# A slot plan for two-way state-space scans: work beside the scans is re-dated, two spare rows go, and GpSimd's order and share change

## The chip, the cores and the metric

The kernel runs on one core of a Trainium2 chip. The metric is the device time of one launch in microseconds. The kernel before took 6414.39 us in the median of three runs (6395.42 to 6419.84). A launch is a whole small network; the change touches one of its nine stages, the state-space layer, which holds about 1900 us of the launch.

The engines are called as the profile calls them: PE is TensorE, DVE VectorE, ACT ScalarE, POOL GpSimd, SP the queue that issues most DMAs.

## The reference

The reference runs a bidirectional Mamba layer (and eight other stages that are not touched) over 32 sequences of 113 tokens with 256 features. Cut to what matters here, for each of the two directions:

```python
xz = x @ in_w.T;  xh, z = split(xz, 2)                  # 512 inner channels each
xc = silu(conv_b + sum(shift(xh, k) * conv_w[:, k] for k in range(4)))
proj = xc @ xproj_w.T                                   # dt (16), B (16), C (16)
delta = softplus(dt @ dt_w.T + dt_b)
dA  = exp(delta[..., None] * A)                         # A = -exp(A_log), 16 states
dBu = (delta * xc)[..., None] * B
h_t = dA_t * h_(t-1) + dBu_t                            # the recurrence, per channel and state
y_t = sum over the 16 states of h_t * C_t
out = ((y + xc * D) * silu(z)) @ out_w.T
```

## The kernel before, in words

Features lie on the 128 partitions. The 32 sequences go in 8 groups of 4, so one row has GT = 4 x 113 = 452 columns. The 512 inner channels make IB = 4 blocks. A group is worked in two *halves*, direction 0 and direction 1, so there are 16 halves, numbered 0 to 15 here; even ones have direction 0. They run in two blocks of code (halves 0 to 7 and 8 to 15), ahead of which a short block prepares the first one.

A half has 16 states of 4 scans each: 64 *slots*. Slot i is block ORDER[i % 4] (0, 2, 1, 3) of state i // 4. Its parts, with the names of the code:

- `decays` (ACT, L1386): dA of the slot, into one of two PSUM banks. ACT can be two slots ahead of the scans.
- `input_terms` (POOL, L1459): dBu = du x B for two blocks at once, 904 columns; two of them a state. That of state n + 1 may begin when the third scan (blocks 0, 1) or the fourth (2, 3) of state n - 1 is done, as dBu has two buffers.
- `recur` (DVE, L1519): the scan. The result of blocks 0 and 1 goes to `hs` in SBUF (two buffers), that of blocks 2 and 3 to one PSUM bank.
- the output products, state x C: blocks 2 and 3 by DVE (`output_term`, L1529), blocks 0 and 1 by POOL (`output_terms`, L1468), 904 columns. A scan into `hs` waits until the product of the state two before is done.
- `product` (PE, L1297): adds the output product to y in PSUM through the identity, in the order of blocks 2, 3, 0, 1: that of state n - 1 at slots 4n to 4n + 3.
- SP loads the rows B and C of a state, broadcast to all partitions, into a ring of four.

Beside the scans, at slots that constants set, each engine does the work that surrounds the recurrence (`beside`). For the half that comes next: X_MM (PE), the convolution's first tap (ACT, TAP), three more taps (DVE), Z_MM (PE), Z_RAW (ACT copies z out of PSUM), SILU twice (ACT: table load, silu of xc, silu of this half's z, table load back), XP_MM and ROWS (B, C and dt), and then four times DT_MM (PE), softplus in three ACT steps, STEP (DVE) and, on POOL, `step_input` (du, L1475). All of these share a single PSUM bank, XZ. For the half before: GATE (DVE), OUT_MM (PE), RES (DVE). Odd halves also normalise the next group (MEAN, CENTRE, SQUARE, VAR, RSTD, SCALE). Every engine takes its list strictly in order, so what waits at a slot holds all later slots of that engine. The last half has no half to prepare.

While ACT is at SILU it can't make dA. Before, two *spare rows* in SBUF (`dA_spare`) are filled ahead of each SILU, for the two slots behind it. So four scans of a half read dA from SBUF; their other operand, dBu, is in SBUF too.

## Time and profile before

| | us |
|---|---|
| median of the runs | 6414.39 |
| the profiled execution's own time | 6388.95 |
| its span | 6387.2 |
| PE busy in the span | 5081.8 |
| DVE busy | 3776.1 |
| ACT busy | 2136.6 |
| POOL busy | 2244.7 |
| the 16 halves: start of the first scan to the end of the last | 1514.8 to about 3341 |

The page gives busy times over all nine stages. Only in the stretch from about 1500 to 3340 us does the changed code run, so shares of the whole span tell little; the rows further down are of that stretch, most of them from two halves in its middle: half 4 (even), whose first scan starts at 1969.87 us, and half 5 (odd), 2085.86 to 2198.63.

### The profile page before, as it was taken

To read this page: it belongs to the slowest core of one execution; us is meant where nothing else is said; L and a number is where in the kernel's file an instruction comes from. 1 tells how busy PE (TensorE), PEld (TensorE's weight loads), DVE (VectorE), ACT (ScalarE), POOL (GpSimd) and SP (SyncE) were. 2 spreads that over 40 slices of the span, in tenths; PEclk is the share of its full clock that TensorE was granted. 3 is DMA by queue.
4 is the path that set the end of the run, shared out by engine and by line. 5 is a ranking of instruction groups with operands and counts; after the bars stand their busy time and mean duration, and the time that the engine had idled before them with its cause. 6 is when DMAs were issued, how large, how long until landed. Compare 5 with 4: busy or idle time off the path is not lost. (4 is left out here: it accounts for less than half of the span.)

```text
span 6387.2 us, 65263 instructions
## 1 busy us (share of the span) xinstructions
PE 5081.8 (80%) x21148; PEld 3347.0 (52%) x21148; DVE 3776.1 (59%) x7281; ACT 2136.6 (33%) x3642; POOL 2244.7 (35%) x1326
## 2 busy tenths in 40 slices
...
DMA packets 154586, 290.22 MB, mean 45 GB/s; under 512 B 24422, under 2 KB 136082, under 8 KB 145520
## 3 DMA queue, kind: packets, MB, share of 16 engines
...
q8 instruction: 115, 1.88, 0.1%
...
## 5 line engine op out<-in xcount | busy, mean ns | idle before, releaser
L1297 PE MATMUL ssm_ps<-ssm_hc,net_ident 128*128 128x452 f32 x2048 | 989.2, 610 | 288.6 <-DVE ssm_hc L1529 236.7
L1459 POOL TENSOR_TENSOR ssm_dBu<-ssm_du,ssm_bc 128x904 f32<-128x904 f32 x512 | 1098.9, 2167 | 21.3 <-DMA ssm_bc<-ssm_rows 11.2
L1297 PEld LDWEIGHTS ssm_ps<-ssm_hc,net_ident 128*128 128x128 f32 x2048 | 399.3, 209 | 827.9 <-DVE ssm_hc L1529 414.0
L1386 ACT ACTIVATE ssm_ps<-ssm_step,ssm_decay 128x448 f32<-128x448 f32 x960 | 597.7, 633 | 639.5 <-DVE ssm_ps L1519 406.9
L2724 POOL TENSOR_TENSOR peer_hot_cols<-peer_hot_cols,peer_codesT 128x512 f32<-128x512 f32 (+1 forms) x240 | 285.4, 1189 | 1162.1 <-DVE peer_hot_cols L2740 1162.1
L1519 DVE TENSOR_TENSOR_SCAN ssm_ps<-ssm_ps,ssm_dBu 128x452 f32<-128x452 f32 x480 | 528.9, 1102 | 115.2 <-ACT ssm_ps L1386 56.4
L1468 POOL TENSOR_TENSOR ssm_hc<-ssm_hs,ssm_bc 128x904 f32<-128x904 f32 x256 | 538.9, 2105 | 89.6 <-DVE ssm_hs L1519 89.4
L1519 DVE TENSOR_TENSOR_SCAN ssm_hs<-ssm_ps,ssm_dBu 128x452 f32<-128x452 f32 x480 | 517.3, 1078 | 56.4 <-ACT ssm_ps L1386 32.1
L2634 PE MATMUL peer_ps<-peer_xn,peer_down 128*128 128x226 f32 x2048 | 452.9, 367 | 23.2 <-issue 16.0
L2737 DVE TENSOR_TENSOR peer_hot_rows<-peer_ramp,peer_codesT 128x1024 f32<-128x1024 f32 (+1 forms) x240 | 282.6, 1177 | 284.2 <-PE peer_ps L2649 254.1
L2649 PEld LDWEIGHTS peer_ps<-peer_hot_cols,peer_hot_rows 128*128 128x128 f32 x3616 | 437.8, 193 | 23.8 <-DVE peer_hot_rows L2737 22.4
L2649 PE MATMUL peer_ps<-peer_hot_cols,peer_hot_rows 128*128 128x64 f32 x3616 | 429.1, 273 | 18.5 <-DVE peer_hot_rows L2737 18.5
L2676 PE MATMUL peer_ps<-peer_hid,peer_up 128*128 128x226 f32 x2048 | 399.7, 355 | 1.5 <-DVE peer_hid L2756 1.5
L2634 PEld LDWEIGHTS peer_ps<-peer_xn,peer_down 128*128 128x128 f32 x2048 | 382.9, 195 | 29.2 <-issue 24.1
L2676 PEld LDWEIGHTS peer_ps<-peer_hid,peer_up 128*128 128x128 f32 x2048 | 390.0, 190 | 6.7 <-issue 2.1
L1529 DVE TENSOR_TENSOR ssm_hc<-ssm_ps,ssm_bc 128x452 f32<-128x452 f32 x512 | 307.5, 601 | 0.0
L418 POOL TENSOR_TENSOR at_ex<-at_ex,at_rs 113x452 f32<-113x452 f32 x128 | 125.3, 982 | 447.7 <-DVE at_rs L470 447.7
L2703 ACT ACTIVATE peer_hid<-peer_ps 128x452 f32<-128x452 f32 x256 | 140.0, 547 | 414.7 <-PE peer_ps L2634 414.7
L2696 ACT ACTIVATE peer_weight<-peer_ps 128x512 f32<-128x512 f32 (+1 forms) x240 | 144.3, 609 | 288.3 <-PE peer_ps L2649 288.3
...
L2421 POOL IOTA peer_ramp<- 128x128 f32 x1 | 0.2, 237 | 636.6 <-ACTq L2410 636.6
L2049 POOL MEMSET rw_back<- 128x4520 f32 x1 | 3.9, 3864 | 592.9 <-POOLq L73 592.9
...
## 6 DMA issues: line engine op xcount, KB each, us to landing
ssm_bc<-ssm_rows SPq DMA_DIRECT2D x256, 452.0 KB, 3.6
...
```

Source lines behind the costliest of these rows:

```text
L1297: nc.tensor.matmul(Y_BANK[j][:, 0:GT], c["ident"][:, :], hc[:, q % 2, j, :], start=False, stop=(n == S - 1))\
L1386: nc.scalar.activation(rows(dA(place[i]))[:, :, lo:lo + N - 1], rows(step[hf.d][:, j, :])[:, :, lo:lo + N - 1], ACT.Exp, scale=decay[hf.d] ...
L1459: nc.gpsimd.tensor_tensor(dBu[:, q % 2, j:j + 2, :], du[hf.d][:, j:j + 2, :], bc[:, q % RING, 0:1, :].to_broadcast([P, 2, GT]), ALU.mult). ...
L1468: nc.gpsimd.tensor_tensor(hc[:, q % 2, 0:2, :], hs[:, q % 2, :, :], bc[:, q % RING, 1:2, :].to_broadcast([P, 2, GT]), ALU.mult).then_inc(s ...
L1519: nc.vector.tensor_tensor_scan(flow(state, hf.d), flow(dA(place[i]), hf.d), flow(dBu[:, q % 2, j, :], hf.d), 0.0, ALU.mult, ALU.add).then_ ...
L1529: nc.vector.tensor_tensor(hc[:, q % 2, j, :], HS_BANK[:, 0:GT], bc[:, q % RING, 1, :], ALU.mult)\
L2634: mm = nc.tensor.matmul(ps[1 + i % 3][:, jj * PT:(jj + 1) * PT], down[:, m, i * J + jj, :], xn[:, m, :], start=(m == 0), stop=(m == DK - 1))
L2649: mm = nc.tensor.matmul(ps[4 + ch % HB][:, t * PB * EB:(t + 1) * PB * EB], hot_rows[:, at % HB, t, :], hot_cols[:, at % HB, t, :], start=T ...
L2676: mm = nc.tensor.matmul(ps[5 + m][:, 0:PT], w_up[:, j, m * P:(m + 1) * P], hid[:, j, :], start=(j == 0), stop=(j == EB - 1))
L2696: nc.scalar.activation(weight[:, :, :, t0:t0 + n], ps[4 + ch % HB][:, 0:n * PB * EB].rearrange("p (t b j) -> p j b t", b=PB, j=EB), ACT.Co ...
L2724: nc.gpsimd.tensor_tensor(hot_cols[:, at % HB, 0:n, :], hot_cols[:, at % HB, 0:n, :], codesT[:, 2, t0:t0 + n].unsqueeze(2).to_broadcast([P ...
L2737: nc.vector.tensor_tensor(hot_rows[:, at % HB, 0:n, :], ramp[:, :].unsqueeze(1).to_broadcast([P, n, P]), codesT[:, 0, t0:t0 + n].unsqueeze ...
```

## The change

Six things change, all in `mamba`.

1. The constants: nearly all beside work gets another slot. GATE moves from 2, 3, 5, 6 to 2, 3, 4, 5; OUT_MM from 8, 11 to 6, 9; RES from 10, 13 to 9, 12; X_MM from 14 + 7m to 13 + 6m; TAP from 16 + 7m to 15 + 6m; Z_MM from 19 + 7m to 16 + 6m; Z_RAW from 21 + 7m to 18 + 6m; SILU from 30, 41 to 27, 36; XP_MM from 44 to 38; DT_MM from 47 + 4m to 42 + 4m; STEP from 50 + 4m to 45 + 4m.
2. `dA_spare` goes. The slots alternate between the two PSUM banks, and ACT works them in their order.
3. The three DVE taps of a block, one a slot before, are issued at one slot.
4. Softplus' three ACT steps, one behind another at one slot before, get a slot each (ABS, EXP, LOG).
5. POOL does the two input products of state n + 1 ahead of the output product of state n - 1, and `step_input` follows states 12 and 14.
6. The output products of states 5, 7 and 8 for blocks 0 and 1 are DVE's (`output_pair`, at slots 26, 35, 36), and PE waits for them on a semaphore of their own, `hc_own`.

```diff
-    MEAN, CENTRE, SQUARE, VAR, RSTD, SCALE = -1, 1, 3, 5, 7, 9
-    GATE = (2, 3, 5, 6)
-    OUT_MM, RES = (8, 11), (10, 13)
-    X_MM = [14 + 7 * m for m in range(IB)]
...
+    MEAN, CENTRE, SQUARE, VAR, RSTD, SCALE = -1, 0, 2, 3, 5, 8
+    GATE = (2, 3, 4, 5)
+    OUT_MM, RES = (6, 9), (9, 12)
+    X_MM = [13 + 6 * m for m in range(IB)]
+    TAP = [15 + 6 * m for m in range(IB)]
+    Z_MM = [16 + 6 * m for m in range(IB)]
+    Z_RAW = [18 + 6 * m for m in range(IB)]
+    SILU = (27, 36)
+    XP_MM, ROWS = 38, 40
+    DT_MM = [42 + 4 * m for m in range(IB)]
+    ABS, EXP, LOG = ([42 + k + 4 * m for m in range(IB)] for k in (1, 2, 3))
+    STEP = [45 + 4 * m for m in range(IB)]
+    DU = {12: 0, 14: 2}
+    PAIR_SLOT = {26: 5, 35: 7, 36: 8}
+    OWN = sorted(PAIR_SLOT.values())
...
+        def pairs(q):
+            own = q // S * len(OWN) + sum(n <= q % S for n in OWN)
+            return q + 1 - own, own
+        def pair_wait(eng, q):
+            pool, own = pairs(q)
+            if q % S in OWN:
+                eng.wait_ge(s["hc_own"], own)
+            else:
+                eng.wait_ge(s["hc_pool"], pool)
...
                         if j < 2:
-                            pe.wait_ge(s["hc_pool"], q + 1)
+                            pair_wait(pe, q)
...
                         for n in range(S):
-                            if hf.rec and n:
-                                output_terms(hf, n - 1)
-                            elif hf.carried is not None:
-                                output_terms(hf.carried, S - 1)
                             if hf.rec and n + 1 < S:
                                 input_terms(hf, n + 1, 0)
                                 input_terms(hf, n + 1, 2)
...
+                            if hf.rec and n:
+                                if n - 1 not in OWN:
+                                    output_terms(hf, n - 1)
+                            elif hf.carried is not None:
+                                output_terms(hf.carried, S - 1)
+                            if n in DU and hf.front:
+                                step_input(hf, DU[n])
...
+                    def output_pair(hf, n):
+                        q = S * hf.r + n
+                        dve.wait_ge(s["scan_done"], IB * q + AT[1] + 1)
+                        if q >= 2:
+                            dve.wait_ge(s["y_pool"], 2 * (q - 1))
+                        nc.vector.tensor_tensor(hc[:, q % 2, 0:2, :], hs[:, q % 2, :, :],
+                                                bc[:, q % RING, 1:2, :].to_broadcast([P, 2, GT]), ALU.mult).then_inc(s["hc_own"], 1)
```

The lists show three places. On PE, around the fourth Z_MM of a half, before (`ssm_w_in` at L1343 is Z_MM, `net_ident` is `product`, waiting for `hc_dve` or `hc_pool`):

```order
L1297 MATMUL ssm_ps<-ssm_hc,net_ident 128x452 [waits ssm_hc_pool] x2
L1297 MATMUL ssm_ps<-ssm_hc,net_ident 128x452 [waits ssm_hc_dve]
L1343 MATMUL ssm_ps<-ssm_ln_out,ssm_w_in 128x452 [waits ssm_conv_step]
L1343 MATMUL ssm_ps<-ssm_ln_out,ssm_w_in 128x452
L1297 MATMUL ssm_ps<-ssm_hc,net_ident 128x452 [waits ssm_hc_dve]
```

and in the changed kernel (Z_MM is L1348, `product` L1302; the X_MM in front of it is L1341):

```order
L1341 MATMUL ssm_ps<-ssm_ln_out,ssm_w_in 128x452 [waits ssm_z_raw]
L1341 MATMUL ssm_ps<-ssm_ln_out,ssm_w_in 128x452
L1302 MATMUL ssm_ps<-ssm_hc,net_ident 128x452 [waits ssm_hc_dve] x2
L1302 MATMUL ssm_ps<-ssm_hc,net_ident 128x452 [waits ssm_hc_own]
L1348 MATMUL ssm_ps<-ssm_ln_out,ssm_w_in 128x452 [waits ssm_conv_step]
L1348 MATMUL ssm_ps<-ssm_ln_out,ssm_w_in 128x452
L1302 MATMUL ssm_ps<-ssm_hc,net_ident 128x452 [waits ssm_hc_own]
```

The fourth Z_MM now stands behind a product that waits for DVE's own pair of state 7, which DVE issues at slot 35.

On ACT, around the second SILU, before (L1386 is `decays`, L1408 is Z_RAW):

```order
L1386 ACTIVATE ssm_ps<-ssm_step,ssm_decay 128x4x112 [waits ssm_scan_done] x4
L1386 ACTIVATE ssm_dA_spare<-ssm_step,ssm_decay 128x4x112 [waits ssm_scan_done] x2
L1413 ACT_TABLE_LOAD [waits ssm_conv_step]
L1413 ACTIVATE ssm_xc<-ssm_conv 128x904
L1418 ACTIVATE ssm_z<-ssm_z 128x904
L1420 ACT_TABLE_LOAD
L1408 ACTIVATE ssm_z<-ssm_ps 128x452 [waits ssm_z_mm]
```

and now (`decays` is L1391, Z_RAW L1413):

```order
L1391 ACTIVATE ssm_ps<-ssm_step,ssm_decay 128x4x112 [waits ssm_scan_done] x3
L1413 ACTIVATE ssm_z<-ssm_ps 128x452 [waits ssm_z_mm]
L1418 ACT_TABLE_LOAD [waits ssm_conv_step]
L1418 ACTIVATE ssm_xc<-ssm_conv 128x904
L1423 ACTIVATE ssm_z<-ssm_z 128x904
L1425 ACT_TABLE_LOAD
L1391 ACTIVATE ssm_ps<-ssm_step,ssm_decay 128x4x112 [waits ssm_scan_done] x4
```

The fourth Z_RAW has moved from behind the second SILU to ahead of it, and nothing is made ahead for the slots behind.

On POOL, from the end of state 4 on, before (L1459 are inputs, L1468 outputs):

```order
L1468 TENSOR_TENSOR ssm_hc<-ssm_hs,ssm_bc 128x904 [waits ssm_y_pool,ssm_scan_done]
L1459 TENSOR_TENSOR ssm_dBu<-ssm_du,ssm_bc 128x904 [waits ssm_scan_done,ssm_landed2] x2
L1468 TENSOR_TENSOR ssm_hc<-ssm_hs,ssm_bc 128x904 [waits ssm_y_pool,ssm_scan_done]
L1459 TENSOR_TENSOR ssm_dBu<-ssm_du,ssm_bc 128x904 [waits ssm_scan_done,ssm_landed3] x2
L1468 TENSOR_TENSOR ssm_hc<-ssm_hs,ssm_bc 128x904 [waits ssm_y_pool,ssm_scan_done]
L1459 TENSOR_TENSOR ssm_dBu<-ssm_du,ssm_bc 128x904 [waits ssm_scan_done,ssm_landed0] x2
```

and now (L1464 inputs, L1473 outputs):

```order
L1464 TENSOR_TENSOR ssm_dBu<-ssm_du,ssm_bc 128x904 [waits ssm_scan_done,ssm_landed2] x2
L1473 TENSOR_TENSOR ssm_hc<-ssm_hs,ssm_bc 128x904 [waits ssm_y_pool,ssm_scan_done]
L1464 TENSOR_TENSOR ssm_dBu<-ssm_du,ssm_bc 128x904 [waits ssm_scan_done,ssm_landed3] x2
L1464 TENSOR_TENSOR ssm_dBu<-ssm_du,ssm_bc 128x904 [waits ssm_scan_done,ssm_landed0] x2
L1473 TENSOR_TENSOR ssm_hc<-ssm_hs,ssm_bc 128x904 [waits ssm_y_pool,ssm_scan_done]
```

Each output now follows the two inputs that it led before, and where DVE has taken a pair, four inputs stand together.

## Rows read from the trace of the kernel before

**Rows 1.** Busy time by engine: halves 4, 5 and 15 (PE, PEld, DVE, ACT, POOL, clock).
```profile
1969.87:2085.86 115.99, 89.83 (x201) 38.17 (x202) 104.08 (x122) 60.53 (x94) 103.96 (x51) 0.91 0.21 65
2085.86:2198.63 112.77, 91.89 (x208) 38.90 (x206) 103.97 (x126) 62.60 (x97) 106.46 (x51) 0.94 0.21 67
3236.18:3341.00 104.82, 73.18 (x152) 30.30 (x152) 96.53 (x108) 48.12 (x70) 102.03 (x49) 0.89 0.18 58
```
**Rows 2.** The page's costliest groups: busy, mean ns | idle before, by releaser.
```profile
L1459 POOL TENSOR_TENSOR ssm_dBu<-ssm_du,ssm_bc 128x904 f32<-128x904 f32 x512 | 1098.9, 2167 | 21.3 <-DMA ssm_bc<-ssm_rows 11.2
...
L1519 DVE TENSOR_TENSOR_SCAN ssm_ps<-ssm_ps,ssm_dBu 128x452 f32<-128x452 f32 x480 | 528.9, 1102 | 115.2 <-ACT ssm_ps L1386 56.4
```
**Rows 3.** Scans from the spare rows into PSUM: ns min/median/max.
```profile
L1519 DVE TENSOR_TENSOR_SCAN ssm_ps<-ssm_dA_spare,ssm_dBu x32: 2202/2660/8458, 1563.7 to 3309.6; 128x452 f32<-128x452 f32 x32
```
**Rows 4.** Timeline (start, us, engine) of half 4, state 11, DVE and POOL.
```profile
2055.89 1.10 DVE L1519 TENSOR_TENSOR_SCAN ssm_hs<-ssm_ps,ssm_dBu 128x452 f32<-128x452 f32 x1 [0.86 <-ACT ssm_ps L1386]
...
2057.07 2.10 POOL L1468 TENSOR_TENSOR ssm_hc<-ssm_hs,ssm_bc 128x904 f32<-128x904 f32 x1 [0.84 <-DVE ssm_hs L1519]
...
2057.64 1.11 DVE L1519 TENSOR_TENSOR_SCAN ssm_ps<-ssm_ps,ssm_dBu 128x452 f32<-128x452 f32 x1
...
2060.38 1.11 DVE L1519 TENSOR_TENSOR_SCAN ssm_ps<-ssm_ps,ssm_dBu 128x452 f32<-128x452 f32 x1
```
**Rows 5.** Timeline: first scans of states 4, 6 and 10 of half 4, and state 4 of half 5.
```profile
1997.47 1.07 DVE L1519 TENSOR_TENSOR_SCAN ssm_hs<-ssm_ps,ssm_dBu 128x452 f32<-128x452 f32 x1
...
2010.31 1.09 DVE L1519 TENSOR_TENSOR_SCAN ssm_hs<-ssm_ps,ssm_dBu 128x452 f32<-128x452 f32 x1
...
2044.48 1.08 DVE L1519 TENSOR_TENSOR_SCAN ssm_hs<-ssm_ps,ssm_dBu 128x452 f32<-128x452 f32 x1
...
2115.57 1.07 DVE L1519 TENSOR_TENSOR_SCAN ssm_hs<-ssm_ps,ssm_dBu 128x452 f32<-128x452 f32 x1
```
**Rows 6.** Timeline of half 4 around a scan from a spare row.
```profile
2018.33 4.21 POOL L1459 TENSOR_TENSOR ssm_dBu<-ssm_du,ssm_bc 128x904 f32<-128x904 f32 x2
...
2021.59 6.01 DVE L1519 TENSOR_TENSOR_SCAN ssm_ps<-ssm_dA_spare,ssm_dBu 128x452 f32<-128x452 f32 x1
...
2024.49 2.14 POOL L1459 TENSOR_TENSOR ssm_dBu<-ssm_du,ssm_bc 128x904 f32<-128x904 f32 x1
```
**Rows 7.** The norm's DVE product of two SBUF rows, 904 columns: ns min/median/max.
```profile
L142 DVE TENSOR_TENSOR ssm_ln_out<-ssm_ln_centred,ssm_ln_rstd x8: 1100/2709/2721, 1442.1 to 3025.5; 128x904 f32<-128x904 f32 x8
```
**Rows 8.** Timeline of half 5: a tap, a product, Z_MM and Z_RAW after an idle PE.
```profile
2145.79 0.66 DVE L1538 SCALAR_TENSOR_TENSOR ssm_conv<-ssm_ps,ssm_conv_w,ssm_conv 128x440 f32<-128x440 f32 x1
...
2145.92 1.88 PE L1297 MATMUL ssm_ps<-ssm_hc,net_ident 128*128 128x452 f32 x2 [5.66 <-DVE ssm_hc L1529]
...
2147.59 2.35 PE L1343 MATMUL ssm_ps<-ssm_ln_out,ssm_w_in 128*128 128x452 f32 x4
...
2149.78 1.68 PE L1297 MATMUL ssm_ps<-ssm_hc,net_ident 128*128 128x452 f32 x4
...
2149.98 0.55 ACT L1408 ACTIVATE ssm_z<-ssm_ps 128x452 f32<-128x452 f32 x1 [1.84 <-PE ssm_ps L1343]
```
**Rows 9.** Timeline of half 5: start of a SILU on ACT, and what follows it.
```profile
2159.53 1.28 ACT L1413 ACT_TABLE_LOAD   x1
...
2163.94 0.55 ACT L1408 ACTIVATE ssm_z<-ssm_ps 128x452 f32<-128x452 f32 x1
```
**Rows 10.** Timeline of half 5: DT_MM and the first softplus step; decays beside it.
```profile
2170.24 1.02 PE L1359 MATMUL ssm_ps<-ssm_dt_in,ssm_w_dt 17*128 17x452 f32 x2
...
2170.71 0.64 ACT L1386 ACTIVATE ssm_ps<-ssm_step,ssm_decay 128x448 f32<-128x448 f32 x1 [0.66 <-DVE ssm_hs L1519]
...
2171.38 0.55 ACT L1434 ACTIVATE ssm_ln_square<-ssm_ps 128x452 f32<-128x452 f32 x1
```
**Rows 11.** Timeline of half 4: OUT_MM.
```profile
1990.93 3.20 PE L1319 MATMUL ssm_ps<-ssm_yz,ssm_w_out 128*128 128x452 f32 x8
```
**Rows 12.** Timeline of half 4: a wait of DVE behind softplus.
```profile
2067.92 1.11 DVE L1519 TENSOR_TENSOR_SCAN ssm_ps<-ssm_ps,ssm_dBu 128x452 f32<-128x452 f32 x1 [1.86 <-ACT ssm_ps L1386]
```

More of the change, by code:

```diff
@@ L1135, in mamba @@
     GATES = (2, 3, 0, 1)
-    MEAN, CENTRE, SQUARE, VAR, RSTD, SCALE = -1, 1, 3, 5, 7, 9
-    GATE = (2, 3, 5, 6)
-    OUT_MM, RES = (8, 11), (10, 13)
-    X_MM = [14 + 7 * m for m in range(IB)]
-    TAP = [16 + 7 * m for m in range(IB)]
-    CONV = [15 + 7 * m for m in range(IB)]
-    Z_MM = [19 + 7 * m for m in range(IB)]
-    Z_RAW = [21 + 7 * m for m in range(IB)]
-    SILU = (30, 41)
-    XP_MM, ROWS = 44, 45
-    DT_MM = [47 + 4 * m for m in range(IB)]
-    SOFTPLUS = [48 + 4 * m for m in range(IB)]
-    STEP = [50 + 4 * m for m in range(IB)]
-    SPARE_ZERO = 50
-    ahead = {i + 1 + k: 2 + k for i in SILU for k in range(2)}
-    place, previous, taken = [], [], {}
-    for i in range(SLOTS):
-        where = ahead[i] if i in ahead else (i - sum(j < i for j in ahead)) % 2
-        place.append(where)
-        previous.append(taken.get(where))
-        taken[where] = i
-    zeroed = {2: -2, 3: -2, place[SLOTS - 2]: -1, place[SLOTS - 1]: 0}
+    MEAN, CENTRE, SQUARE, VAR, RSTD, SCALE = -1, 0, 2, 3, 5, 8
[13 more added lines that the diff above has]
+    OWN = sorted(PAIR_SLOT.values())
     scratch = nc.dram_tensor("ssm_rows", [2, 2, S, GT], F32).ap()
@@ L1181, in mamba @@
         mag = norm.square
-        dA_spare = st.sbuf("dA_spare", [P, 2, GT])
         bc = st.sbuf("bc", [P, RING, 2, GT])
@@ L1242, in _ @@
             def _(dve):
-                for k in range(4):
+                for k in range(2):
                     nc.vector.memset(starts(k, 0), 0.0)
@@ L1441, in _ @@
                         for i in range(SLOTS):
-                            if hf.rec and i not in ahead:
+                            if hf.rec:
                                 decays(hf, i)
-                            if hf.rec and i in SILU:
-                                decays(hf, i + 1)
-                                decays(hf, i + 2)
                             beside(hf, i)
@@ L1517, in recur @@
                             if q >= 2:
[L1518 to L1519 removed]
+                                pair_wait(dve, q - 2)
+                        nc.vector.tensor_tensor_scan(flow(state, hf.d), flow(dA(i % 2), hf.d), flow(dBu[:, q % 2, j, :], hf.d),
                                                      0.0, ALU.mult, ALU.add).then_inc(s["scan_done"], 1)
```

59 lines of the change are left out of this document (28 added, 31 removed).

## The prediction

> **What bounds the kernel now.** I read the busy times by stretch first. In half 4 DVE and POOL are both busy for 104 of 115.99 us, in half 5 for 104.0 and 106.5 of 112.77, ACT for only about 61 and PE for 90 [rows 1]. So a half is bound by two engines that wait for each other in turn, and what counts is who is late at which slot. The page's groups give the unit prices [rows 2]: a scan 1.10 us, a POOL product 2.17. The timeline gives the pace: scans 2057.64 and 2060.38 are two slots apart, 2.74 us with one output product between; a state costs DVE 5.48 us [rows 4]. The scan at 2055.89 is the third of its state, and POOL starts 1.18 us later [rows 4]. One state's three POOL products, 2.1 each where nothing is in their way [rows 4, 6], take 6.2 us: more than DVE's 5.48. But before this has not bound, since DVE also does the beside work and is held up by other things: scans from the spare rows take 2.66 us in the median and up to 8.46 where they go to PSUM [rows 3], and ACT is late behind softplus [rows 12].
>
> I give times within a half from its first scan; s(i) is the start of scan i. Before, half 4 has s(16) = 27.60, s(24) = 40.44, s(40) = 74.61, end 115.99; half 5 has s(16) = 29.71 [rows 1, 5].
>
> **What the parts remove.** Spare rows: 64 scans wait for POOL. The 32 into PSUM are 1.56 us over a normal scan in the median [rows 2, 3], 50 us in all, more by the long ones; with the 32 others I take 100. POOL loses three products of 2.1 a half. Softplus' waits (1.86 us in the longest shown) have their cause in three ACT steps at one slot; with one step (0.55 for the first) and one `decays` of 0.64 a slot [rows 10], ACT needs 1.2 to 1.3 us where DVE takes 1.37: hidden, if the matmul is in time. These are real gains, near 10 us a half if nothing else were late.
>
> **What they add.** Three taps at once depend on one another: a tap of 0.66 us [rows 8] followed by a dependent one costs 0.8 by my estimate, the last 0.58, 2.2 us together; spread, they hid partly in the gap behind an output product (0.4 to 0.57 each). That is +0.8 us a block, +3 a half. A DVE pair has both inputs in SBUF. The nearest row is the norm's product of the same size: 1.10 us alone, 2.71 beside POOL [rows 7]; 1.1 and 6.0 (a scan that lost POOL's queue twice) are the ends. I take 2.7 for state 5 and 1.1 to 3.5 for 7 and 8. Cover: they stand around the SILUs, when DVE would wait for dA anyway.
>
> **POOL's order.** The output of state n - 1 may start, now as before, 1.18 us after s(4n - 2), but two inputs go first: it is done at s(4n - 2) + 7.4 at the earliest, before at + 3.3. PE wants it at slot 4n + 2, which DVE reaches at s(4n - 2) + 5.5. So from now on PE is 1.9 us late at each third slot of a state, and whatever stands right behind (DT_MM, OUT_MM, Z_MM at such slots) is late too. DVE's own scans stay fed: the scan that needs this product's buffer starts at s(4n - 2) + 8.25 (six slots), 0.85 us of slack; before it was over 3.
>
> **The ledger of an even half**, taking each slot's start as the latest of DVE free, dA, dBu and buffers, with the durations above, a product on PE at 0.84 (1.68 for two [rows 8]), OUT_MM at 3.2 [rows 11]:
> - Slots 0 to 16. OUT_MM at slot 6 stands behind product(0, block 0), which waits for POOL until 12.4; two matmuls on, it runs from 14.2 to 17.4. DVE is at RES (slot 9) by 15.5: 1.9 us of wait. The second (slot 9) has three products and 3.2 us ahead of it: RES at 24.0 instead of 22.3. X_MM follows only after the four products of slots 10 to 13 (3.4) and 1.8, the first tap on ACT 0.8: DVE waits 1.6 more. s(16) = 32.1: **+4.5**.
> - Slots 16 to 24: 5.5, and 5.5 + 2.2 for taps: 13.2 against 12.84, **+0.4**.
> - Slots 24 to 40. First SILU: the conv step is through at s(25) + 3.4, SILU holds ACT 4.41 [rows 9], decays 0.64: s(28) = s(25) + 8.5. DVE has scans, the pair at 2.7 and taps to do in 8.4 of it: hidden. State 7 costs 5.5, then s(32) to s(35) 6.7. Then the second SILU. The pair of state 7 is issued at slot 35, behind scan 35, and is done at P = s(35) + 2.6 at best. PE has been idle since slot 33; slot 34's product waits for P; Z_MM stands behind it; Z_RAW (slot 36) waits for Z_MM; it stands on ACT ahead of SILU, and SILU ahead of dA of slot 37. After an idle of 5.66 us, from the product's start to Z_RAW's start were 4.06 us [rows 8]. So s(37) = P + 0.1 + 4.06 + 0.5 + 4.41 + 0.7 = P + 9.8. DVE has in the meantime scan 36, one output product and the pair of state 8, 3.1 us: it idles 6.7. s(40) - s(24) = 38.5 against 34.17: **+4.3**, though the spare scans are gone from it. If DVE's pair loses the queue to POOL's next product, as the 6.01 us scan did [rows 6], 2.06 more.
> - Slots 40 to 64. DT_MM (slots 42 + 4m) stands behind product(n - 1, block 0), hence behind POOL's output, done at E. ABS starts 1.14 us after DT_MM [rows 10]: s(next state) = E + 0.1 + 0.84 + 1.14 + 0.57 + 0.64 = E + 3.3, where 2.75 after its own slot was wanted. By states this makes waits of 2.4, 0.3, 1.7 and 2.2 us, in the place of the three or so waits of 1.1 to 1.9 before; then POOL, with du (2 x 2.06), ends the half at 125.7. 41.9 against 41.38: **+0.5**.
>
> Even: 125.7 against 116.0, **+9.7**. Odd halves: MEAN (slot -1) stands behind the last half's POOL product, CENTRE moved to slot 0 waits 2.2 us for it, SCALE 2.7 as before [rows 7]: s(16) = 33.2 against 29.71, then as above 93.6 against 83.06: 126.8 against 112.8, **+14.0**. Half 0 has no output nor norm: +4. Half 15 has no front: the spare scans' loss (one of 8.46 us [rows 3]) goes, POOL's 6.2 a state, RES and the pairs come: +4, from 104.82 [rows 1]. I price the other even halves as half 4 and the odd ones as half 5.
>
> Sum: 7 x 14 + 7 x 9.7 + 4 + 4 = 174; half a lost turn (1 us) in 15 halves: +15. On the profiled execution's own time, 6388.95: 6578. The three runs' median lies 25.4 above that execution; their mean with it is 16 above, which I add: about **6590**, +2.8%.
>
> **A rule weighed.** The spare scan of 6.01 us began 0.85 us ahead of the end of the POOL product then running (4.21 us for two from 2018.33), and saw two more POOL products go first, the last from 2024.49 [rows 6]. The Trainium skill, SBUF — State Buffer, Who interferes with whom, says that a DVE instruction with two SBUF inputs contends with GpSimd's reads, and that whoever starts first has the port pair for a whole instruction while the other is blocked. The trace agrees that they contend, yet by that rule a pair would wait for one product at most; the sum would then be 6575, by the row up to 6590 and, with every pair of state 7 losing, 6605.
>
> **The rivals.**
> - *Contention gone, waits hidden (faster).* The spare scans' 100 us go, softplus' waits, 4 us a half, go too, taps and uncovered pairs give back 45 + 65: about 6389 - 100 - 60 + 110 = 6340. For it: DVE's busy time would fall, POOL's too. Against: it needs PE to be in time with Z_MM at slot 34 and DT_MM, and the list puts both behind late products. It decides if PE's wait is short of the slack of 0.9 us that ACT has. Chance 0.09; 0.04 for this cancelling to within 0.5%.
> - *Only the second SILU is late (slower, less).* PE catches up elsewhere and waits at RES, CENTRE and DT_MM stay as before: +4.3 in evens, +9 in odds, 6389 + 100 = 6490. Chance 0.17.
> - *The pairs starve.* All three lose POOL's queue, and the 0.85 us of slack breaks, so that DVE takes POOL's 6.2 us for more states: 3 to 5 us a half more, 6640 to 6680. Chance 0.12.
> - The forecast, 6520 to 6630: 0.58.
>
> A measurement of this kernel tells 0.5% from no change, 32 us. Faster 0.09, same 0.04, slower 0.87. Ends of the costs and the milder case taken in, the range is 6440 to 6660.
>
> **What would show it.** In the profile after: a DVE idle of about 6 us before scan 37 of a half, put down to ACT's `decays`, and ACT idle before Z_RAW for PE; PE idle before products released by the pair or by POOL's output; ABS waiting for DT_MM; scans all 1.1 us; the pairs 1.1 to 3.5 us; POOL busy about 97 to 100 us of a half of 125. If halves last under 112 us, the forecast is wrong, and the step that failed is the one from POOL's order to PE's lateness; if the last 24 slots alone are shorter than 41 us, it is the DT_MM step.

## The result, and the profile after

| | before | after |
|---|---|---|
| median, us | 6414.55 (6395.42 to 6419.84, 4 runs) | 6606.6 (6586.56 to 6629.11, 4 runs) |
| ratio, 95% interval | 1 | 1.0306 [1.0267, 1.0345] |
| profiled execution's own time | 6388.95 | 6605.47 |
| its span | 6387.2 | 6603.7 |
| the 16 halves, start of the first scan to the end of the last | 1825.4 | 2024.7 |

The changed kernel is 3.1% slower; 6590 was forecast. In the profiled executions the span grew by 216.5 us, and the 16 halves by 199.4. The last scan of before ends at 3340.20; the stretches to 3341.00 that are shown, here and in [rows 1], run 0.8 us past it. The rest lies outside the halves: the state-space layer began 35 us later, the block that prepares its first half took 3 more, and what is behind the halves took 21 less.

The busy times by stretch: the 16 halves of before, then of after, and after's halves 4, 5 and 15, which answer to [rows 1] (PE, PEld, DVE, ACT, POOL, clock).

```profile
1514.82:3341.00 1826.18, 1436.07 (x3184) 607.56 (x3184) 1645.07 (x1945) 969.89 (x1500) 1678.87 (x797) 0.91 0.21 65
```
```profile
1552.77:3577.50 2024.73, 1542.52 (x3181) 637.04 (x3182) 1649.54 (x1958) 961.16 (x1500) 1566.24 (x749) 0.86 0.19 59
2061.05:2187.50 126.45, 96.58 (x201) 40.07 (x201) 102.76 (x124) 59.90 (x94) 97.91 (x48) 0.86 0.20 60
2187.50:2317.03 129.53, 100.41 (x209) 41.40 (x209) 105.47 (x126) 61.96 (x97) 98.88 (x48) 0.87 0.19 58
3477.71:3577.50 99.79, 75.93 (x155) 33.74 (x156) 92.42 (x106) 47.82 (x69) 91.05 (x44) 0.85 0.22 65
```

DVE's busy time is the same over the 16 halves (1645 and 1650 us), POOL's is 113 less, yet the stretch is 199 longer: the engines wait. On DVE two terms nearly cancel: the 64 scans from spare rows had taken 107 us more than 1.1 us each, and the 48 pairs take 88. From half 1 to half 14 an even half takes 126.4 to 127.2 us and an odd one 129.1 to 129.6, but for half 7, on whose end the second block of code begins: 139.0, and 124.4 before. Half 15, which prepares nothing, is the only one that got shorter (104.0 to 99.8).

The page's groups, which answer to [rows 2]:

```profile
L1464 POOL TENSOR_TENSOR ssm_dBu<-ssm_du,ssm_bc 128x904 f32<-128x904 f32 x512 | 1077.5, 2125 | 457.5 <-DVE ssm_hs L1521 411.0
L1521 DVE TENSOR_TENSOR_SCAN ssm_ps<-ssm_ps,ssm_dBu 128x452 f32<-128x452 f32 x512 | 565.7, 1105 | 171.0 <-ACT ssm_ps L1391 116.4
L1521 DVE TENSOR_TENSOR_SCAN ssm_hs<-ssm_ps,ssm_dBu 128x452 f32<-128x452 f32 x512 | 554.1, 1082 | 160.8 <-ACT ssm_ps L1391 130.5
```

POOL idled 21 us ahead of its inputs before and idles 457 now; all scans are normal ones (1.08 to 1.11 us); and they wait for ACT 247 us in sum, where it was 89 before. What ACT waited for is seen in the timeline of half 4 around its second SILU (start, us, engine):

```profile
2128.00 1.52 DVE L1540 TENSOR_TENSOR ssm_hc<-ssm_hs,ssm_bc 128x904 f32<-128x904 f32 x1
2129.58 1.87 PE L1302 MATMUL ssm_ps<-ssm_hc,net_ident 128*128 128x452 f32 x2 [6.40 <-DVE ssm_hc L1540]
...
2131.25 2.40 PE L1348 MATMUL ssm_ps<-ssm_ln_out,ssm_w_in 128*128 128x452 f32 x4
...
2133.69 0.55 ACT L1413 ACTIVATE ssm_z<-ssm_ps 128x452 f32<-128x452 f32 x1 [6.68 <-PE ssm_ps L1348]
2134.25 1.28 ACT L1418 ACT_TABLE_LOAD   x1
...
2139.39 1.11 DVE L1521 TENSOR_TENSOR_SCAN ssm_ps<-ssm_ps,ssm_dBu 128x452 f32<-128x452 f32 x1 [6.95 <-ACT ssm_ps L1391]
```

This is the chain of the prediction, link by link: the pair of state 7 ends at 2129.5; PE, idle for 6.40 us, does the product and then Z_MM; Z_RAW starts 4.11 us after the product did (4.06 before [rows 8]); SILU follows, and DVE has waited 6.95 us at scan 37 (6.7 forecast). And around the first DT_MM:

```profile
2145.74 2.09 POOL L1473 TENSOR_TENSOR ssm_hc<-ssm_hs,ssm_bc 128x904 f32<-128x904 f32 x1
...
2147.88 1.88 PE L1302 MATMUL ssm_ps<-ssm_hc,net_ident 128*128 128x452 f32 x2 [2.06 <-POOL ssm_hc L1473]
...
2149.69 1.87 PE L1364 MATMUL ssm_ps<-ssm_dt_in,ssm_w_dt 17*128 17x452 f32 x2
...
2151.59 0.55 ACT L1438 ACTIVATE ssm_ln_square<-ssm_ps 128x452 f32<-128x452 f32 x1 [4.95 <-PE ssm_ps L1364]
...
2152.76 1.10 DVE L1521 TENSOR_TENSOR_SCAN ssm_hs<-ssm_ps,ssm_dBu 128x452 f32<-128x452 f32 x1 [4.04 <-ACT ssm_ps L1391]
```

POOL's output product stands behind two inputs and ends at 2147.8; PE's product and DT_MM then take 1.88 and 1.87 us, where before a DT_MM took 1.02 [rows 10]; DVE waits 4.04 us at scan 44. Why PE is slow there is seen in the stretches: first PE's busy time, last but two the granted clock; the changed kernel's product and DT_MM behind the idle time, a stretch of it ahead of that, and before's DT_MM.

```profile
2147.88:2151.60 3.72, 3.72 (x5) 1.11 (x5) 0.83 (x1) 0.01 (x1) 3.72 (x2) 0.50 0.43 124
2140.00:2144.00 4.00, 1.83 (x4) 0.37 (x3) 3.87 (x5) 2.91 (x5) 2.38 (x2) 1.00 0.06 14
```
```profile
2170.24:2171.30 1.06, 1.06 (x4) 0.34 (x3) 0.96 (x2) 0.59 (x1) 0.54 (x1) 1.00 0.26 96
```

PE had been busy for 1.83 of 4 us, at a clock of 1.00 (2.4 GHz); in its wait of 2.06 us for POOL the granted clock is 0.63 in the mean, so it fell while PE idled; behind it PE is granted 0.50 (1.2 GHz), and takes nearly twice as long. Before, DT_MM stood behind a busy PE and ran at 1.00. In the odd half, MEAN stands behind the last half's POOL product, and CENTRE waits:

```profile
2190.59 1.74 PE L107 MATMUL ssm_ps<-net_h,net_ones 128*128 128x452 f32 x4
...
2192.38 1.10 DVE L135 TENSOR_TENSOR ssm_ln_centred<-net_h,ssm_ps 128x904 f32<-128x904 f32 x1 [3.26 <-PE ssm_ps L107]
```

The DVE products with both inputs in SBUF, the pairs and SCALE [rows 7] (ns min/median/max):

```profile
L1540 DVE TENSOR_TENSOR ssm_hc<-ssm_hs,ssm_bc x48: 1239/1523/2757, 1596.7 to 3537.5; 128x904 f32<-128x904 f32 x48
...
L142 DVE TENSOR_TENSOR ssm_ln_out<-ssm_ln_centred,ssm_ln_rstd x8: 1100/2077/2087, 1477.2 to 3240.0; 128x904 f32<-128x904 f32 x8
```

The pair of state 5 takes 2.75 us in every half, that of state 7 1.52 and that of state 8 1.24. None of them, nor SCALE, waited for more than one product of POOL: the rival in which the pairs starve did not come about here.

### The profile page after: what moved, and what is told of

Its sections match the earlier page's. It is cut to its first block and busy times, and to the rows that moved or that the text cites. A ratio compares the mean times of both kernels' runs of the same rounds, so it can differ in the third digit from the quotient of the medians.

```text
span 6603.7 us, 65253 instructions
## 1 busy us (share of the span) xinstructions
PE 5180.6 (78%) x21148; PEld 3368.9 (51%) x21148; DVE 3788.2 (57%) x7295; ACT 2129.4 (32%) x3642; POOL 2137.2 (32%) x1278
## 3 DMA queue, kind: packets, MB, share of 16 engines
q8 instruction: 115, 1.88, 0.1%
## 5 line engine op out<-in xcount | busy, mean ns | idle before, releaser
L1302 PE MATMUL ssm_ps<-ssm_hc,net_ident 128*128 128x452 f32 x2048 | 1064.8, 649 | 460.1 <-POOL ssm_hc L1473 196.5
L1464 POOL TENSOR_TENSOR ssm_dBu<-ssm_du,ssm_bc 128x904 f32<-128x904 f32 x512 | 1077.5, 2125 | 457.5 <-DVE ssm_hs L1521 411.0
L1302 PEld LDWEIGHTS ssm_ps<-ssm_hc,net_ident 128*128 128x128 f32 x2048 | 414.5, 219 | 1063.2 <-issue 343.1
L1391 ACT ACTIVATE ssm_ps<-ssm_step,ssm_decay 128x448 f32<-128x448 f32 x1024 | 645.7, 635 | 655.6 <-DVE ssm_ps L1521 371.1
L1521 DVE TENSOR_TENSOR_SCAN ssm_ps<-ssm_ps,ssm_dBu 128x452 f32<-128x452 f32 x512 | 565.7, 1105 | 171.0 <-ACT ssm_ps L1391 116.4
L1521 DVE TENSOR_TENSOR_SCAN ssm_hs<-ssm_ps,ssm_dBu 128x452 f32<-128x452 f32 x512 | 554.1, 1082 | 160.8 <-ACT ssm_ps L1391 130.5
L1473 POOL TENSOR_TENSOR ssm_hc<-ssm_hs,ssm_bc 128x904 f32<-128x904 f32 x208 | 443.0, 2130 | 3.6 <-DVE ssm_hs L1521 3.6
L2646 PEld LDWEIGHTS peer_ps<-peer_xn,peer_down 128*128 128x128 f32 x2048 | 381.3, 194 | 28.8 <-issue 24.0
L2752 DVE TENSOR_TENSOR peer_hot_cols<-peer_ramp,peer_codesT 128x512 f32<-128x512 f32 (+1 forms) x240 | 203.2, 847 | 0.0
## 6 DMA issues: line engine op xcount, KB each, us to landing
ex_w<-in_l_ffn_w SPq DMA_DIRECT2D x66, 1024.0 KB, 10.4
peer_down<-in_peer_down_t SPq DMA_DIRECT2D x1, 4096.0 KB, 16.4
```

The lines of the kernel that those rows point to most:

```text
L1302: nc.tensor.matmul(Y_BANK[j][:, 0:GT], c["ident"][:, :], hc[:, q % 2, j, :], start=False, stop=(n == S - 1))\
L1391: nc.scalar.activation(rows(dA(i % 2))[:, :, lo:lo + N - 1], rows(step[hf.d][:, j, :])[:, :, lo:lo + N - 1], ACT.Exp, scale=decay[hf.d][:, ...
L1464: nc.gpsimd.tensor_tensor(dBu[:, q % 2, j:j + 2, :], du[hf.d][:, j:j + 2, :], bc[:, q % RING, 0:1, :].to_broadcast([P, 2, GT]), ALU.mult). ...
L1473: nc.gpsimd.tensor_tensor(hc[:, q % 2, 0:2, :], hs[:, q % 2, :, :], bc[:, q % RING, 1:2, :].to_broadcast([P, 2, GT]), ALU.mult).then_inc(s ...
L1521: nc.vector.tensor_tensor_scan(flow(state, hf.d), flow(dA(i % 2), hf.d), flow(dBu[:, q % 2, j, :], hf.d), 0.0, ALU.mult, ALU.add).then_inc ...
L2646: mm = nc.tensor.matmul(ps[1 + i % 3][:, jj * PT:(jj + 1) * PT], down[:, m, i * J + jj, :], xn[:, m, :], start=(m == 0), stop=(m == DK - 1))
```

## The experiments

The experiments ran in three sets (e1 to e4, e5 to e8, e9 to e12). Each set had its own runs of the kernel before on the same chip (medians 6388.52, 6378.51 and 6387.94 us), so kernels of different sets are compared by their ratios to it. One ratio point (0.01) is 64 us.

**e1: the pair of state 7 early.** The pair stands at slot 31, right behind the scan of its second block, not at 35.

```diff
-    PAIR_SLOT = {26: 5, 35: 7, 36: 8}
+    PAIR_SLOT = {26: 5, 31: 7, 36: 8}
```

> The changed kernel with DVE's own pair of state 7 issued at slot 31 instead of 35. My theory (PE's list puts Z_MM of slot 34 behind the product that waits for this pair, Z_RAW behind Z_MM, SILU behind Z_RAW, dA of slot 37 behind SILU): the wait of DVE before scan 37 falls from 6.95 us to about 2, the pair at slot 31 is no longer covered and costs 1.2 to 2.7, so a half is 2 to 4 us shorter and the launch about 30 to 60 us faster than the changed kernel. Rival (the wait is SILU's own length, whoever stands in front of it): the wait stays above 5 us and the launch gains nothing or loses the uncovered pair, up to 40 us slower.

Measured: 6491.42 us, ratio 1.0156 [1.0116, 1.0196], some 96 us faster than the changed kernel, more than expected. The waits of half 4 before scans 37 and 44:

```profile
2084.41 1.11 DVE L1521 TENSOR_TENSOR_SCAN ssm_ps<-ssm_ps,ssm_dBu 128x452 f32<-128x452 f32 x1 [1.32 <-ACT ssm_ps L1391]
2097.78 1.10 DVE L1521 TENSOR_TENSOR_SCAN ssm_hs<-ssm_ps,ssm_dBu 128x452 f32<-128x452 f32 x1 [4.04 <-ACT ssm_ps L1391]
```

6.95 became 1.32 (2.91 in half 5), and the DT wait stayed at 4.04. So the second SILU's delay comes from the pair's slot, and the DT delay doesn't. Part of the gain is lost again further on: the wait at scan 56 of half 4 is 3.26 us, where the changed kernel has 0.38.

**e2: POOL's outputs first.** As the changed kernel, but the output product of state n - 1 goes ahead of the inputs of state n + 1 again.

```diff
+                            if hf.rec and n:
+                                if n - 1 not in OWN:
+                                    output_terms(hf, n - 1)
+                            elif hf.carried is not None:
+                                output_terms(hf.carried, S - 1)
                             if hf.rec and n + 1 < S:
                                 input_terms(hf, n + 1, 0)
                                 input_terms(hf, n + 1, 2)
...
-                            if hf.rec and n:
-                                if n - 1 not in OWN:
-                                    output_terms(hf, n - 1)
-                            elif hf.carried is not None:
-                                output_terms(hf.carried, S - 1)
```

> The changed kernel with POOL's order of before: the output product of state n - 1 ahead of the input products of state n + 1. My theory (late outputs make PE late, and with it ABS, RES and CENTRE): the waits before slots 44 to 56 (7.8 us in half 4) fall under 2, those at RES (2.0) under 1.2, CENTRE's 3.3 in half 5 under 1.5; halves 4 and 5 take about 117 and 119 us instead of 126.5 and 129.5, and the launch is 120 to 160 us faster than the changed kernel. Rival (the second SILU's chain is the whole loss, the POOL order costs nothing): gain under 40 us.

Measured: 6500.2 us, ratio 1.0187 [1.0164, 1.021], some 76 us faster than the changed kernel, less than expected. In half 4:

```profile
2062.23 1.11 DVE L1521 TENSOR_TENSOR_SCAN ssm_ps<-ssm_ps,ssm_dBu 128x452 f32<-128x452 f32 x1 [7.77 <-ACT ssm_ps L1391]
2074.02 1.10 DVE L1521 TENSOR_TENSOR_SCAN ssm_hs<-ssm_ps,ssm_dBu 128x452 f32<-128x452 f32 x1 [2.46 <-ACT ssm_ps L1391]
```

The DT wait fell to 2.46 and those at slots 52 and 56 went; the wait at 37, which belongs to the pair, even grew. RES of half 4 no longer waited for OUT_MM, and CENTRE of half 5 waited 1.38 us, both as expected. Half 4 took 119.14 us, half 5 126.63 (117 and 119 were expected): in the odd halves SCALE now took 5.06 us in the median where it had taken 2.08, and that ate part of the gain.

**e3: both.** The edits of e1 and e2 together.

> Both edits: POOL's outputs first and the pair of state 7 at slot 31. My theory: the gains add, halves 4 and 5 take 113 to 116 us, and the launch is near the kernel before or up to 60 us faster than it (6350 to 6420). Rival (contention of the DVE pairs or the taps at once is what costs): still over 60 us slower than the kernel before.

Measured: 6412.41 us, ratio 1.0042 [1.0025, 1.0059]. The two gains, 1.50 and 1.19 points, add up: 2.69 against the 2.64 measured. The launch came out within what was expected, the halves on both sides of it: even ones took 112 us, odd ones 120 to 123 (half 7 aside), for 113 to 116. SCALE in half 5, with the POOL products around it (DVE's row, then POOL's):

```profile
2089.05 5.33 DVE L142 TENSOR_TENSOR ssm_ln_out<-ssm_ln_centred,ssm_ln_rstd 128x904 f32<-128x904 f32 x1
...
2087.20 2.12 POOL L1473 TENSOR_TENSOR ssm_hc<-ssm_hs,ssm_bc 128x904 f32<-128x904 f32 x1
2089.27 4.15 POOL L1464 TENSOR_TENSOR ssm_dBu<-ssm_du,ssm_bc 128x904 f32<-128x904 f32 x2
```

SCALE started at 2089.05, 0.2 us ahead of the end of a POOL product, let the two behind it pass, and ended at 2094.38, one normal duration behind them.

**e4: POOL's new order in the kernel before.** The inputs of state n + 1 first, then the output of n - 1, at the half's end too, where the output of state 14 fell behind du and the next half's first inputs.

> The kernel before with one edit, POOL's inputs of state n + 1 ahead of the output of state n - 1 (at the end of a half the same). My theory: DT_MM, OUT_MM and MEAN become late in its plan as well, 4 to 8 us a half, so 60 to 120 us slower than before. Rival (inputs first takes away DVE's waits for dBu at a half's start, 1.7 us, and PE's lateness is slack): the same or up to 25 us faster than before.

Measured: 6582.05 us, ratio 1.0307 [1.0279, 1.0334], +194 us where 60 to 120 were expected. Not all of it is from what was meant: at the half's end the output of state 14 came so late that state 15 took 17.4 us, where it took 7.0 before. So it was repeated.

**e5: the same, but outputs first at the last state.** Inputs lead for states 0 to 14 only.

```diff
-                            if hf.rec and n:
+                            if n == S - 1 and hf.rec:
                                 output_terms(hf, n - 1)
-                            elif hf.carried is not None:
-                                output_terms(hf.carried, S - 1)
                             if hf.rec and n + 1 < S:
                                 input_terms(hf, n + 1, 0)
                                 input_terms(hf, n + 1, 2)
+                            if hf.rec and 0 < n < S - 1:
+                                output_terms(hf, n - 1)
+                            elif n == 0 and hf.carried is not None:
+                                output_terms(hf.carried, S - 1)
```

> The kernel before with POOL's inputs of state n + 1 ahead of the output of state n - 1, but the end of a half (last state) left in its old order, so that no output stands behind du there. My theory (late outputs alone make PE, and ACT behind it, late): state 15 is back at 7 us, odd halves stay 5 to 9 us above before and even ones 1 to 3, together 40 to 80 us slower than before. Rival (the former run's loss was only its half end, 17.4 us instead of 7 in state 15): within 15 us of before.

Measured: 6557.48 us, ratio 1.027 [1.0229, 1.031], +172 us where 40 to 80 were expected. The order alone, in the old plan, costs nearly as much as the whole change. Half 4 took 8.3 us more than before (124.3 against 115.99; 1 to 3 were expected for even halves) and half 5 13.4 more (5 to 9 for odd ones). In half 4, at RES of slot 10 and at scan 61:

```profile
2038.18 0.63 DVE L1560 TENSOR_TENSOR net_h<-ssm_ps,net_h 128x452 f32<-128x452 f32 x1 [2.40 <-PE ssm_ps L1319]
...
2135.50 1.11 DVE L1521 TENSOR_TENSOR_SCAN ssm_ps<-ssm_ps,ssm_dBu 128x452 f32<-128x452 f32 x1 [6.00 <-ACT ssm_ps L1386]
```

RES waits 2.40 us for OUT_MM (0.42 before). Scan 61 waits 6.00 us where it had waited 1.21: the product ahead of the last DT_MM waits for POOL, whose order is du, two inputs, and then the output; PE idles 4.80 us meanwhile. This wait lies in state 15, which took 8 to 12 us (half 7 aside) and not the 7 expected. PE's rows there:

```profile
2127.80 3.38 PE L1297 MATMUL ssm_ps<-ssm_hc,net_ident 128*128 128x452 f32 x4 [4.80 <-POOL ssm_hc L1468]
2131.11 1.87 PE L1359 MATMUL ssm_ps<-ssm_dt_in,ssm_w_dt 17*128 17x452 f32 x2
```

DT_MM takes 1.87 us again. In the changed kernel du follows the outputs at states 12 and 14, and half 4 has a wait for ACT of 0.38 us at scan 56 and none behind it. So the same order does not cost the same at the same places in the two plans.

**e6: no spare rows in the kernel before.** `decays` goes slot by slot on the two PSUM banks (what cleared the spare rows' first columns goes with them).

```diff
-    ahead = {i + 1 + k: 2 + k for i in SILU for k in range(2)}
+    ahead = {}
...
-                            if hf.rec and i in SILU:
-                                decays(hf, i + 1)
-                                decays(hf, i + 2)
```

> The kernel before without the spare rows: all slots alternate between the two PSUM banks and ACT makes nothing ahead of a SILU. My theory: the 100 us of port waits of the spare scans go, and two waits of about 4 us a half for ACT at the SILUs come in their place, so within 30 us of before; all scans at 1.1 us. Rival A (port waits are a loss on top): 60 us or more faster. Rival B (the spare rows cover the SILU well): 40 us or more slower.

Measured: 6408.07 us, ratio 1.0049 [1.0034, 1.0064], +31 us, at the slow edge of the 30 us expected. All scans take 1.1 us, so some 100 us of waiting for POOL are gone, but the scans' waits for ACT rose from 89 to 207 us. Behind the first SILU of half 4, for one:

```profile
2039.65 1.11 DVE L1516 TENSOR_TENSOR_SCAN ssm_ps<-ssm_ps,ssm_dBu 128x452 f32<-128x452 f32 x1 [3.20 <-ACT ssm_ps L1386]
```

Behind the second it is 2.51 at scan 42 and 2.01 at scan 46 (0.86 before).

**e7: outputs first and no pairs.** As e2, and POOL does all output products.

```diff
-    PAIR_SLOT = {26: 5, 35: 7, 36: 8}
+    PAIR_SLOT = {}
```

> The changed kernel with POOL's outputs first and no pairs on DVE at all: POOL does all 16 outputs of a half. My theory: DVE loses three products of 1.5 to 2.7 us, mostly in the cover of the SILUs, and POOL, with 103 us of work in halves of about 115, begins to bind behind the SILUs: 10 to 50 us slower than the run with both edits. Rival (the pairs cost DVE more than they give POOL): 10 to 40 us faster than it.

Measured: 6372.38 us, ratio 0.9992 [0.997, 1.0014], 0.5 points under e3, so the rival holds: the pairs cost more than they give, even with the pair of state 7 at slot 31. Now no difference to before can be told.

**e8: e3 with the norm's and the output's slots of before.** Outputs first; MEAN to RES as before, and all behind them a slot later than in the changed kernel, pairs at 27, 32 and 37.

```diff
-    MEAN, CENTRE, SQUARE, VAR, RSTD, SCALE = -1, 0, 2, 3, 5, 8
+    MEAN, CENTRE, SQUARE, VAR, RSTD, SCALE = -1, 1, 3, 5, 7, 9
...
-    SILU = (27, 36)
+    SILU = (28, 37)
```

> POOL's outputs first, the pair of state 7 right behind the output product of slot 32, the norm, GATE, OUT_MM and RES at the slots of the kernel before, and everything from X_MM on one slot later than in the changed kernel. My theory: SCALE at slot 9 asks for the port early in a POOL product and takes 2.1 to 2.7 us instead of 5.1, RES and the taps wait less, so odd halves fall from 120 to 123 us to 113 to 117 and even ones stay at 112: 20 to 60 us faster than the run with both edits and up to 45 us faster than the kernel before. Rival (the odd halves' loss is the three taps at once and X_MM's closeness, not SCALE): gain under 15 us.

Measured: 6468.86 us, ratio 1.0149 [1.0114, 1.0185], a miss: worse than e3, where better than before was expected. The first 16 slots of odd halves were better (30.5 us for about 36), though SCALE took 4.3 us in the median and not 2.1 to 2.7. But state 7 took 12 to 14.5 us where it had taken 7.0 in halves 4 and 5 of e3. The trace shows the chain, here in half 4:

```profile
2024.18 1.02 PE L1302 MATMUL ssm_ps<-ssm_hc,net_ident 128*128 128x452 f32 x2 [3.87 <-DVE ssm_hc L1540]
...
2025.04 2.68 PE L1341 MATMUL ssm_ps<-ssm_ln_out,ssm_w_in 128*128 128x452 f32 x4
...
2028.52 2.11 DVE L1549 SCALAR_TENSOR_TENSOR ssm_conv<-ssm_ps,ssm_conv_w,ssm_conv 128x448 f32<-128x448 f32 x3 [2.65 <-ACT ssm_conv L1406]
```

The product of slot 26 waits for the pair of state 5, now at slot 27, and X_MM, which moved from slot 25 to 26, stands behind this product. So X_MM comes late, ACT's first tap waits for it, DVE's taps wait 1.65 to 4.0 us for ACT at slot 28 in every half, and SILU, behind the tap, makes scan 29 wait 3.0 more. In e3 X_MM stood ahead of the product. It is what Z_MM and the pair of state 7 do in the changed kernel, at another place: one slot more for all changed who stands behind whom.

**e9: taps at once in the kernel before.**

```diff
-                        for m in range(IB):
-                            if CONV[m] < i < CONV[m] + TAPS:
-                                tap(hf, m, i - CONV[m])
+                        if i in TAP:
+                            for t in range(1, TAPS):
+                                tap(hf, TAP.index(i), t)
```

> The kernel before with one edit: the three DVE taps of a block stand together at the slot of the first of them (16 + 7m) instead of one a slot. Theory of the prediction: three taps that depend on one another cost 2.2 us together, spread they hid in part in the gap behind an output product, +0.8 us a block, +3 us a half, 15 halves: about +45 us, ratio 1.007. Rival: ACT and POOL are waited for at these slots anyway, so it is nothing, within 10 us. A second rival: DVE gives back time, since Z_MM is no longer waited for and the scans behind run free, -10 to -40 us.

Measured: 6433.75 us, ratio 1.0071 [1.005, 1.0092], +45 us: the sum that the prediction's term gives. Its spread is another: in the traces odd halves took 1.3 to 7.8 us more than before and even ones from 1.6 less to 3.9 more, not 3 each. So the term's 0.8 us a block isn't shown, and that the sum comes out is in part luck. The three taps of a block in half 4, one behind another:

```profile
2026.68 2.11 DVE L1538 SCALAR_TENSOR_TENSOR ssm_conv<-ssm_ps,ssm_conv_w,ssm_conv 128x448 f32<-128x448 f32 x3 [1.12 <-ACT ssm_conv L1401]
```

2.1 us for the three (2.2 taken), and here a wait of 1.12 for ACT's first tap ahead of them, which half 4 of before doesn't have; over the whole kernel such waits are 37.3 us, 28.8 before, which is 8.5 of the 45.

**e10: e7 with the norm's slots of before.**

```diff
-    MEAN, CENTRE, SQUARE, VAR, RSTD, SCALE = -1, 0, 2, 3, 5, 8
+    MEAN, CENTRE, SQUARE, VAR, RSTD, SCALE = -1, 1, 3, 5, 7, 9
```

> The changed kernel with GpSimd's outputs ahead of its inputs and no pairs on DVE (6372 us, ratio 0.999, in the earlier job), and besides the norm's slots as before: CENTRE at 1, SQUARE 3, VAR 5, RSTD 7, SCALE 9. There the odd halves took 115 to 120 us against 110 for the even ones: CENTRE waited 1.92 us for MEAN, and SCALE, asked for 2.1 us ahead of the end of a POOL product that ran, took 4.46 us or more, with a state of 10.2 to 11.0 us and one of 9.7 to 10.7. Theory: SCALE one slot later lands where the port is free sooner, 2.7 us or 1.1, and CENTRE waits under 0.5: odd halves 112 to 114 us, -5 us each, about -35 us, ratio 0.991 to 0.995. Rival: SCALE loses the port wherever it stands while POOL is nearly full (0.95 of the time); then under 10 us, ratio 0.997 to 1.001.

Measured: 6357.19 us (10 runs), ratio 0.995 [0.9931, 0.997]: faster than before by 0.5%, with e11 the best of all, and at the slow end of what was expected. The expected cause is not what the traces show. The stretches of e10, all 16 halves and halves 4 and 5:

```profile
1518.94:3321.90 1802.96, 1425.36 (x3181) 589.75 (x3182) 1576.55 (x1910) 966.36 (x1500) 1641.82 (x797) 0.94 0.22 66
1970.57:2080.65 110.08, 86.82 (x201) 35.72 (x200) 96.99 (x121) 60.28 (x94) 102.93 (x51) 0.97 0.22 69
2080.65:2195.80 115.15, 93.94 (x209) 39.03 (x208) 101.93 (x122) 61.71 (x96) 103.16 (x51) 0.93 0.22 65
```

CENTRE waits 0.79 us, not 1.92, in half 5; but SCALE took 4.36 us in the median, more than e7's 3.28 (3.83 and 4.46 in half 5). The odd halves took 115 to 119 us (half 7 126.3), in e7 115 to 120, and still lose to before's 112.8. The even ones win, with 110 to 112, as they did in e7. In the traces the 16 halves took 1803.0 us and e7's 1810.1, so most of the step from 0.9992 to 0.995 between the two sets is not explained by them.

**e11: pairs where DVE idles.** As e10, with `PAIR_SLOT = {27: 6, 36: 8}`.

> As e10_norm_slots, and DVE takes the output pairs of states 6 and 8 at slots 27 and 36, right behind the scan that stands ahead of each SILU wait (slots 28 and 37, 2.54 and 3.31 us of idle) and three slots ahead of the product that needs them. Theory: a pair at such a place costs nothing, since DVE idles there, and relieves POOL of two products of 2.1 us; POOL sets the pace of some states only, so 1 to 3 us a half less than e10: -15 to -45 us. Rival: the pair loses the port to POOL's inputs and outlasts the wait (5 us and over), +1 to +2 us a half: +15 to +30 us.

Measured: 6355.2 us, ratio 0.996 [0.9941, 0.9979], not told apart from e10 (0.995). In half 4 the waits at scans 28 and 37 fell from 2.54 and 3.32 us to 0.45 and 1.32, and the halves stayed at 110 to 118 (half 7 126.4): the pairs (2.4 us in the mean, one of them 7.42) fill the wait and no more, and scans wait for POOL instead (1.7 to 2.3 us at scan 56 of these two halves). Neither side came about.

**e12: the changed kernel without pairs.** Inputs first, `PAIR_SLOT = {}`.

> The changed kernel without pairs: POOL does all output products, still behind the inputs. Theory: the pair of state 7 is what makes slot 37 late (6.95 us, state 9 13.5 us), but POOL would now bring that product no sooner than its turn behind two inputs, and it has 3 x 2.1 us more to do a half; the POOL order alone costs what e5_before_inputs_first_b showed (ratio 1.027), so this stays within 0.5% of the changed kernel: ratio to before 1.024 to 1.036. Rival: the pairs are a loss by themselves, as they were with outputs first (0.5%): then the ratio is 1.018 to 1.024, with the wait before scan 37 at 3 to 4 us.

Measured: 6497.07 us, ratio 1.0186 [1.0154, 1.0218], 1.2 points under the changed kernel. The rival holds. In half 4:

```profile
2051.18 1.11 DVE L1521 TENSOR_TENSOR_SCAN ssm_ps<-ssm_ps,ssm_dBu 128x452 f32<-128x452 f32 x1 [3.92 <-ACT ssm_ps L1391]
2064.54 1.10 DVE L1521 TENSOR_TENSOR_SCAN ssm_hs<-ssm_ps,ssm_dBu 128x452 f32<-128x452 f32 x1 [4.04 <-ACT ssm_ps L1391]
```

Scan 37 waits 3.92 us without a pair. With POOL's old order as well (e7) it is 3.31, which is what the SILU costs there; POOL's order adds 0.6, and the pair had added 3. The DT wait is POOL's, again 4.04 (2.34 in half 5).

**The runs as one account.** Going from the changed kernel back to before, in ratio points (the kernels are of three sets, each against its own runs of before): taking the pairs away 1.20 (after to e12), giving POOL its old order 1.94 (e12 to e7), and what is then left is 0.08 faster than before (e7, within its interval). Of 3.06 points, some 196 us, the pairs hold 77 us and the order 124. The rest cancels inside: taps at once cost 0.71 (e9), spare rows given up 0.49 (e6), so the rest (the other slots, softplus' steps apart, du's place) gave back about 1.3. That last number is the difference only and was not run alone. Nor is the account the same in every order: with outputs first the three pairs cost 1.95 points (e2 against e7), and the pair of state 7 at slot 31 costs nothing that can be told with inputs first (e1 against e12, 1.0156 and 1.0186, whose intervals overlap).

## Why the prediction was right, step by step

- **What bounds the kernel.** Right. Neither engine's work sets the time, but who is late at which slot: DVE's work did not change, POOL's fell, the time rose, and DVE and POOL held each other up through PE and ACT.
- **Slots 0 to 16, even half.** 32.1 us forecast, 29.77 measured in half 4. The mechanism is there, the size was too large: RES came 16.4 and 22.4 us into the half, where 17.4 and 24.0 were worked out, behind waits of 0.85 and 1.17 us for OUT_MM, and the first tap waited 0.93 instead of 1.6.
- **Slots 16 to 24.** 13.2 forecast, 12.99 measured.
- **Slots 24 to 40.** 38.5 forecast, 39.33 measured; the wait at scan 37 6.95 for 6.7. It is the pair's slot (e1, e12), as worked out. The rule weighed in the prediction had no occasion to decide: the pair of state 7 never took more than 1.52 us.
- **Slots 40 to 64.** 41.9 forecast, 44.36 measured. This step was mis-sized, at the term for PE: I took 0.84 us for the product and 1.14 from DT_MM to ABS, and behind an idle PE they took 1.8 and 1.9. The wait at scan 44 was 4.04 us instead of 2.4; those at 48, 52 and 56 were 0.56, 2.82 and 0.38, where 0.3, 1.7 and 2.2 were worked out. In e2, with outputs first, the wait at 44 was 2.46 and the other three were gone.
- **Even half.** 125.7 forecast, 126.45 measured: the too large and the too small term cancel, which is luck. Against before it was 10.4 to 10.6 us more in five of the seven, for 9.7; halves 2 and 8 grew by 15 and 16, since before they had been shorter than half 4, as which all were priced.
- **Odd half.** 126.8 forecast, 129.53 measured. CENTRE waited 3.26 us instead of 2.2, for the same reason: ahead of MEAN stand two products on a PE that had idled 3.78 us, and they took 3.2 us, where two take 1.68 in [rows 8]. The other part is the DT term.
- **Halves 0 and 15.** Half 0 took 8.6 us more, 4 were forecast. Half 15 took 4.2 less (99.8 for 104.0) where 4 more were forecast: the sign was wrong. It has no front, so no Z_MM, SILU of a next half or DT_MM stands behind POOL's products or the pairs, and what is left is the gain from the spare scans: e6, which drops only these, takes 99.7 us for it. I had priced POOL's 6.2 us a state there; e7, with the old order and no pairs, takes 98.2 us for it against 99.8, so the new order and the pairs together cost 1.6 us where no such work hangs on them.
- **Lost turns.** 15 us were added for pairs that wait for one POOL product more; none did. The odd halves' shortfall stands in its place. In sum 189 us were forecast for the halves, and 199.4 measured. Another 17 us of the profiled execution's growth came from outside the halves, which nothing in the prediction speaks of; and the 16 us added to get from that execution to the median were 1 us in the changed kernel. That 6590 stands so near 6606.6 is owed in part to such errors of either sign.
- **The rivals.** "Contention gone" had its gain real but paid for (e6). "Only the second SILU is late" would have been half the truth: e1, without that delay, is still 1.6% slower than before. The pairs did not starve in the changed kernel, though in e2 and e3 one took 6.6 us, in e8 and e11 one 7.4, and SCALE up to 5.4.

The size of the order alone was expected too small, 40 to 80 us in the old plan, where e5 measured 172. I had counted how late POOL's product is, and neither du in its queue ahead of it nor the slow matmuls behind the longer idle time of PE.
